# Cross-attention block with feed-forward on one core: a third pair of keys leads, and the start of the attention stage is ordered anew

## The reference, cut to what matters

```python
h = layernorm(x)                                   # (8, 128, 512)
q = rmsnorm(h, ln_weight) @ w_q.T                  # 32 heads x 128
k, v = ctx @ w_k.T, ctx @ w_v.T
score = einsum('bqhd,bkhd->bhqk', q, k) + position_bias[None]
p = softmax(where(mask, score, -inf)); p = where(mask, p, 0)
x = x + h + einsum('bhqk,bkhd->bqhd', p, v) @ w_out.T
xf = layernorm(x)                                  # then the routed feed-forward
x = x + (xf * in_scale) @ sign(weight).T * out_scale + bias
```

## Time and profile before

| | us |
|---|---|
| median of 3 runs | 875.49 (874.83 to 876.92) |
| the profiled execution, its own time | 873.7 |
| its span | 871.9 |
| TensorE busy | 843.1 |
| VectorE / ScalarE / GpSimd busy | 633.6 / 389.2 / 288.1 |

### The profile page before, as it was taken

One profiled execution on the slowest core, in us unless ns is written; L12 is line 12 of the kernel. 1 busy time (PEld: TensorE's weight loads), 2 busy tenths in 40 slices (PEclk: granted clock), 3 DMA queues, 4 the chain that ended last, 5 costly groups with the idle time before them and its releaser, 6 DMA issues.

```text
span 871.9 us, 12869 instructions
## 1 busy us (share of the span) xinstructions
PE 843.1 (97%) x4348; PEld 706.0 (81%) x4348; DVE 633.6 (73%) x1019; ACT 389.2 (45%) x1005; POOL 288.1 (33%) x279
## 2 busy tenths in 40 slices
PE   9889999999899998799999999999999999999897
PEld 8778888888778876688888888888888888888775
DVE  5966746846877696777777777777777787789755
ACT  5623413413332352445544554555555445556542
POOL 0211111111011024244545445544454355433236
PEclk9999999999999999999999999999999999999969
DMA  8173553555453648242144224413431342150002
GB/s 305 68 230 121 184 202 109 174 213 157 151 170 133 204 145 277 103 148 98 58 151 149 66 89 148 142 49 116 148 105 66 135 149 97 59 206 7 1 0 97
DMA packets 58656, 114.07 MB, mean 131 GB/s; under 512 B 5192, under 2 KB 34760, under 8 KB 53344
## 3 DMA queue, kind: packets, MB, share of 16 engines
q1 hardware_dynamic: 58592, 113.25, 37.7%
HBM read 77.58 MB, written 35.65 MB: 130 GB/s over the span
## 4 chain that ended last, share of the span: by engine, by line
PE 79%; DVE 11%; DMA 3%; ACT 3%; issue 2%; POOL 1%; SPq 0%; POOLq 0%; DVEq 0%; ACTq 0%
PE out L1207 9%; PE out L1209 9%; PE out L1208 9%; PE proj L1207 8%; PE proj L1209 8%; PE proj L1208 8%; PE o L1298 6%; PE s L1279 6%; PE t L1287 3%; PE s L1207 3%; PE s L1209 3%; PE s L1208 2%; DVE w_lo L941 2%; DMA w_stage<-in_wk 2%; DMA w_stage<-in_wq 2%
## 5 line engine op out<-in xcount | busy, mean ns | idle before, releaser
L815 ACT ACTIVATE probs<-probs,neg_max 128x128 f32<-128x128 f32 x256 | 99.8, 391 | 145.4 <-DVE neg_max L1074 145.3
L667 POOL TENSOR_TENSOR w_stage<-w_stage 128x256 f32<-128x256 f32 x30 | 22.5, 749 | 342.5 <-DMA w_stage<-in_wk 275.2
L1097 DVE TENSOR_TENSOR acc<-out,acc 128x512 f32<-128x512 f32 x128 | 87.4, 688 | 41.7 <-PE out L1209 41.1
L679 POOL TENSOR_TENSOR w_lo<-w_stage,w_hi 128x512 fp32r<-128x512 f32 (+1 forms) x52 | 60.0, 1165 | 135.0 <-ACT w_hi L753 135.0
L1207 PE MATMUL out<-wo_hi,o_hi 128*128 128x512 f32 x224 | 95.2, 425 | 0.7 <-DVE acc L1097 0.6
L1207 PE MATMUL proj<-x_hi,w_hi 128*128 128x512 f32 x210 | 88.9, 423 | 2.0 <-DVE w_lo L941 1.5
L1209 PE MATMUL out<-wo_lo,o_hi 128*128 128x512 f32 x224 | 88.0, 393 | 0.0
L1208 PE MATMUL out<-wo_hi,o_lo 128*128 128x512 f32 x224 | 87.6, 391 | 0.0
L1209 PE MATMUL proj<-x_lo,w_hi 128*128 128x512 f32 x210 | 82.5, 393 | 0.0
L1208 PE MATMUL proj<-x_hi,w_lo 128*128 128x512 f32 x210 | 82.1, 391 | 0.0
L753 ACT ACTIVATE w_hi<-w_stage 128x512 fp32r<-128x512 f32 (+1 forms) x113 | 62.0, 566 | 39.7 <-POOL w_stage L669 26.2
(11 more groups left out here) (317 smaller groups left out, 2130.0 us busy)
## 6 DMA issues: line engine op xcount, KB each, us to landing
k_spill<-ring SPq DMA_DIRECT2D x64, 256.0 KB, 2.8
v_spill<-ring SPq DMA_DIRECT2D x64, 256.0 KB, 2.2
w_stage<-in_wk SPq DMA_DIRECT2D x32, 256.0 KB, 3.1
big_stage<-in_wv SPq DMA_DIRECT2D x8, 1024.0 KB, 8.2
w_stage<-in_wq SPq DMA_DIRECT2D x32, 256.0 KB, 4.1
k_first<-k_spill SPq DMA_DIRECT2D x8, 1024.0 KB, 7.1
v_first<-v_spill SPq DMA_DIRECT2D x8, 1024.0 KB, 4.8
k_second<-k_spill SPq DMA_DIRECT2D x8, 1024.0 KB, 7.1
```

The costliest lines, as they stand in the source:

```text
L679: pool.tensor_tensor(lo, w_stage[:, STAGED[part]], hi.bitcast(F32), ALU.subtract).then_inc(g_wlo, 1)
L815: last = act.activation(probs[:, j % 2, b, :], probs[:, j % 2, b, :], ACT.Exp, bias=neg_max[:, col:col + 1], accum_out=row_sum[:, col:col ...
L1097: dve.tensor_tensor(acc[:, b, :], out_bank[n % 2][:], acc[:, b, :], ALU.add).then_inc(v_acc, 1)
```

## The change

It touches the order of steps and a few buffers. Nothing is computed in another way.

- **A third pair of keys leads:** the groups are K0 K1 K2, then V V K V V K K three times, then the last four value groups in a row, then K12 to K15 and the queries. Loads, sums and splits of pair 2 move ahead of the values' load and splits.
- **Two staged blocks have two places:** `w_stage` has ten blocks; for odd pairs the second block of row 1 and the last sum lie in 8 and 9 instead of 6 and 7. Row 1 of pair m now waits for the sums of pair m - 1 and for part 3 of pair m - 2; GpSimd's sums wait for part 2 of pair m - 1.
- **Value sums are own steps** (VS, g, n), in three slots; **roots are own steps** of ScalarE (LNR, RMSA), behind LN and RMS by some slots.
- **x:** H writes into the x tile itself; x loads 4 to 7 wait for transposes 0 to 3. Transposes 0 to 3 stand beside the first of the last value groups. Keys and values of pair 0 are loaded in cycle 30 instead of 31.
- **The first units:** score 1, transpose 0 and EXP 1 stand inside cycle 33; units 1 to 4, with the products of groups 33 and 34 beside them, have an order written out.
- **Memory:** `bias_raw` moves behind `probs`; its first two loads wait for the x splits.

```diff
-    order = KEYS[0:2]
-    for g in range(NVG):
-        k = 2 + 3 * g
+    order = KEYS[0:3]
+    for g in range(NVG - 1):
+        k = 3 + 3 * g
...
-    return order + KEYS[14:] + QUERIES
+    return order + VALUES[-HALF:] + KEYS[-4:] + QUERIES
...
-        k = weights_at(m)
-        near = m > 0 and weights_at(m - 1) == k - 1
-        if m:
-            put(k, 4 if near else 1, ("WX", m + 1, 0))
+        near = m > PLAIN and weights_at(m - 1) == weights_at(m) - 1
+        k = weights_at(m) + {PLAIN: 2, PLAIN + 1: 1}.get(m, 0)
+        put(k, 4 if near else 1, ("WX", m + 1, 0))
         put(k, 6 if near else 5, ("WX", m + 1, 1))
         put(k + 1, 1, ("WX", m + 1, 2))
         if m <= NPAIR:
-            put(k + 1, 0, ("WL", m + 2, 0))
-        put(k + 1, 2, ("WX", m + 1, 3))
-        if m <= NPAIR:
-            put(k + 1, 2, ("WL", m + 2, 1))
-            put(k + 1, 4, ("WS", m + 2))
...
+            put(k + 1, 0, ("WL", m + 2, 1), ("WL", m + 2, 0))
+            put(k + 1, 3, ("WS", m + 2))
+        put(k + 1, 5 if m == NPAIR else 2, ("WX", m + 1, 3))
+
+    put(2, 0, ("VS", 0, 2))
+    put(2, 2, ("VX", 0, 6))
+    put(2, 4, ("WX", 2, 3), ("WL", 3, 1), ("WL", 3, 0))
+    put(2, 6, ("VX", 0, 2))
+    put(3, 0, ("CT", "T4"), ("CX", 4))
+    put(3, 2, ("VX", 0, 5))
+    put(3, 4, ("VS4", 0), ("VX", 0, 7))
+    put(4, 0, ("WS", 3), ("VX", 0, 3))
+    put(4, 2, ("VX", 0, 4))
+    put(4, 4, ("VL", 1))
+    put(6, 0, ("VS", 1, 0))
+    put(6, 3, ("VS", 1, 1))
+    put(6, 6, ("VS", 1, 2))
...
-    put(k - 6, 6, ("LN", 0))
-    put(k - 5, 1, ("RMS", 0))
-    put(k - 5, 4, ("RMSR", 0))
...
+    put(k - 7, 2, ("LN", 0))
+    put(k - 7, 6, ("LNR", 0))
+    put(k - 6, 1, ("RMS", 0))
+    put(k - 6, 4, ("RMSA", 0))
+    put(k - 6, 6, ("RMSR", 0))
...
+    for i in range(HALF):
+        put(k, i, ("X", i), ("XL", HALF + i))
+    put(k, 6, ("LN", 1))
+    put(k + 1, 2, ("LNR", 1))
...
+    put(k + 4, 0, ("XX", 1))
+    put(k + 4, 2, ("XT", "T1"), ("XX", 2))
+    put(k + 4, 5, ("XT", "T2"), ("XX", 7))
...
+    put(k + 6, 5, ("KV", 0), ("BL", 0), ("BL", 1))
+    q = at[QUERIES[0]]
+    put(q, 5, ("BM", 0), ("BM", 1))
+    put(q, 6, ("KV", 1), ("WOL", 0))
+
+    put(q + 1, 0, ("S", 0), ("EXP", 0), ("SMALL",))
+    put(q + 1, 3, ("N", 0), ("BL", 2))
+    put(q + 1, 4, ("S", 1))
+    put(q + 1, 6, ("T", 0), ("EXP", 1), ("BM", 2))
...
+             ("WX", 2, 0), *plain_read(1, "C11"), ("WX", 2, 1), *plain(1, "C12", 0), *plain(1, "C12", 1), ("CX", 5), *plain_read(1, "C21"),
+             ("WX", 2, 2), *plain(1, "C22", 0), *plain(1, "C22", 1), ("VX", 0, 1), ("VS", 0, 0), ("VS", 0, 1), ("CX", 7),
+             *plain_read(1, "C12"), *plain_read(1, "C22")]
...
-            steps += slot(j, product(first, 7) + prod[1], product(first, 3), [], [("WX", m, 2)])
-            steps += slot(j + 1, prod[6] + product(first, 4), prod[2], [("WO", p)], [("WX", m, 3)])
...
+            steps += [*product(first, 7), *prod[1], ("WX", m, 2), ("N", 1), ("PV", 0), ("RES", 0), ("RES", 1)]
+            steps += [("S", 2), *product(first, 3), ("T", 1), ("EXP", 2), ("BM", 3), ("BL", 3), *prod[6], ("N", 2), ("PV", 1),
+                      ("WO", 0), ("RES", 2), ("RES", 3)]
+            steps += [("S", 3), *product(first, 4), *prod[2], ("WX", m, 3), ("T", 2), ("EXP", 3), ("BM", 4), *prod[5], ("N", 3),
+                      ("PV", 2), ("WOL", 1), *load, ("RES", 4), ("RES", 5)]
+            steps += [("S", 4), *prod[7], *prod[3], ("T", 3), ("EXP", 4), ("BM", 5), ("BL", 4), ("RES", 6), ("RES", 7), *prod[4],
+                      *outs(0, 0), ("N", 4), ("KV", 2), *sums, ("PV", 3), *outs(0, 1, 2)]
...
+                else:
+                    sp.wait_ge(g_wsum, 4 * (m - PLAIN))
+                if m > PLAIN and row == 0:
                     sp.wait_ge(*low_done(m - 1, 0))
                     sp.wait_ge(*low_done(m - 1, 1))
-                    sp.wait_ge(g_wsum, 4 * (m - PLAIN))
-                else:
-                    sp.wait_ge(*low_done(m - 1, 2))
-                    sp.wait_ge(*low_done(m - 1, 3))
...
+                if m > PLAIN + 1 and row == 1:
+                    sp.wait_ge(*low_done(m - 2, 3))
...
+                    to = w_stage[:, 5:9:3] if m % 2 else w_stage[:, 5:7]
...
             def x_load(i):
                 if i >= HALF:
-                    sp.wait_ge(v_hs, i - HALF + 1)
+                    sp.wait_ge(pe_x, i - HALF + 1)
...
+                if m > PLAIN:
+                    pool.wait_ge(*low_done(m - 1, 2))
```

More of the change, by code:

```diff
@@ new lines, in schedule @@
+            put(k + 5, 5, ("VS", g + 1, 1))
+            put(k + 6, 1, ("VS", g + 1, 2))
+    k = at[VALUES[-HALF]]
+    put(k - 9, 3, ("ML",))
+    put(k - 9, 5, *[("XL", i) for i in range(HALF)])
+    put(k - 8, 3, ("MASK",))
+    put(k - 7, 2, ("LN", 0))
[3 more added lines that the diff above has]
+    put(k - 6, 6, ("RMSR", 0))
+    put(k - 5, 2, ("H", 0))
+    put(k - 5, 5, ("H", 1))
+    put(k - 4, 1, ("H", 2))
+    put(k - 4, 5, ("H", 3))
@@ new lines, in schedule @@
+    for i in range(HALF):
+        put(k, i, ("X", i), ("XL", HALF + i))
+    put(k, 6, ("LN", 1))
+    put(k + 1, 2, ("LNR", 1))
+    put(k + 1, 3, ("RMS", 1))
+    put(k + 1, 5, ("RMSA", 1))
+    put(k + 2, 0, ("RMSR", 1))
+    put(k + 2, 2, ("H", 4))
+    put(k + 2, 4, ("H", 5))
+    put(k + 2, 5, ("X", 4))
+    put(k + 2, 6, ("H", 6))
+    put(k + 3, 0, ("X", 5))
+    put(k + 3, 1, ("H", 7))
+    put(k + 3, 2, ("X", 6))
+    put(k + 3, 4, ("X", 7), ("AL",))
+    put(k + 3, 6, ("XT", "T3"))
@@ L485, in split_tiles, with staged @@
             return w_hi[:, PARTS[part]], w_lo[:, PARTS[part]]
+        def staged(m, part):
+            if part == 3:
+                return w_stage[:, 8:10] if m % 2 else w_stage[:, 6:8]
+            return w_stage[:, (slice(0, 1), slice(1, 3), slice(3, 5))[part]]
         def ctx_low_done(i):
@@ L615, in bias_load @@
             def bias_load(i):
-                if i >= 2:
+                if i < 2:
+                    sp.wait_ge(a_xhi, 7)
+                    sp.wait_ge(v_xlo, 7)
+                else:
                     sp.wait_ge(g_bm, max(j for j in range(len(UNITS)) if bias_of(j) == i - 2) + 1)
@@ L678, in query_weights_low @@
                 pool.wait_ge(a_whi, nth_split[m, part])
-                pool.tensor_tensor(lo, w_stage[:, STAGED[part]], hi.bitcast(F32), ALU.subtract).then_inc(g_wlo, 1)
+                pool.tensor_tensor(lo, staged(m, part), hi.bitcast(F32), ALU.subtract).then_inc(g_wlo, 1)
             def bias_and_mask(j):
@@ L746, in weights_high @@
                     before = m - 2
-                if before < PLAIN:
+                if m == PLAIN:
+                    act.wait_ge(pe_plain, all_plain // 2 if part < 2 else nth_plain[1, part - 2, 0, 1])
+                elif before < PLAIN:
                     act.wait_ge(pe_plain, all_plain)
@@ L752, in weights_high @@
                             act.wait_ge(pe_prod, nth_product[group_with(before), i])
-                act.activation(hi, w_stage[:, STAGED[part]], ACT.Copy).then_inc(a_whi, 1)
+                act.activation(hi, staged(m, part), ACT.Copy).then_inc(a_whi, 1)
             def values_high(g, i):
@@ L940, in key_weights_low @@
                 dve.wait_ge(a_whi, nth_split[m, part])
-                dve.tensor_tensor(lo, w_stage[:, STAGED[part]], hi.bitcast(F32), ALU.subtract).then_inc(v_wlo, 1)
+                dve.tensor_tensor(lo, staged(m, part), hi.bitcast(F32), ALU.subtract).then_inc(v_wlo, 1)
             def values_low(g, i):
@@ L1039, in normed @@
                 dve.wait_ge(v_hs, i + 1)
[L1040 to L1044 removed]
+                dve.scalar_tensor_tensor(out=x_tiles[:, i % HALF, :], in0=hs_tile, scalar=rrms[:, i:i + 1],
                                          in1=lnw_bc, op0=ALU.mult, op1=ALU.mult).then_inc(v_h, 1)
```

120 lines of the change are left out of this document (36 added, 84 removed).

## The result

The changed kernel takes **870.28 us** (median of eight runs, 868.79 to 873.62), the kernel before 876.66 on the same chip (872.78 to 877.90). The ratio is 0.9943, 95% interval 0.9921 to 0.9964: faster, by 6.4 us (0.7%) in the medians. The forecast was 858 with a range of 854 to 868, so the sign was right and the gain was a third of what I had worked out.

What follows compares the result with a forecast made beforehand. TensorE, busy 97% of the span, was taken as the bound, so only its idle time could go: 22.7 us at most, less 4.9 lost anew, gives 17.8. From 873.7 that is 855.9 profiled, 858 median, range 854.3 to 868.

Steps and rivals of the forecast that it cites:

- The 22.7 us that could be won: Ceiling on the gain: TensorE's waits ahead of 385 us, with restarts and slow clock, in the profiled execution before.
- The start: Third key pair leading: 1.6 us lost as VectorE has no slack and meets GpSimd's pair sums (bounds 0.4 and 4).
- The waits of the value sums: Later value groups: with sums in separate slots, the 2.5 us wait for E65 and two short waits (0.9) go.
- the root: ScalarE's root, moved 3 to 4 slots after its source, no longer holds up E1; TensorE's 2.5 us loss goes.
- The new wait of the pair sums: Rival, attention stage: later sums make each of 14 pairs' weights late, 22 us come back, 880 us; chance 0.03.
- land 9.5 to 10 later ... 1.0 lost (bounds 0 and 3): First query product: weight rows of pair 16, queued behind 2 MB of keys and values, cost 1.0 us.
- the loads behind keys and values come late: Rival: 2 more at the first query, 3 more at unit 0, 1.7 of clock, 864.5 us; chance 0.12.
- Walking it from the start of group 33 ... I take 1.5 lost; bounds 0.4 and 6: First attention units in their new order: small waits, a late load and restarts cost 1.5 us.
- By hand E65 of it ends 0.9 ahead of need. I leave 0.1; keep 2 as the upper bound.: Group 28, x sums and splits pushed together on VectorE: its read E65 still in time, 0.1 us lost.
- both middle rivals: VectorE becomes the bound in pressed stretches (863.5 us, chance 0.18); loads behind keys and values late (864.5, chance 0.12).
- over 8 us of waits ahead of 385: Sign in the changed profile: TensorE waits totalling more than this before 385 us would show the forecast wrong.
- a wait of over 1 us after 400: Sign in the changed profile: one such TensorE wait would show the forecast wrong.

Runs made afterwards that it cites:

- e8: The kernel before with value sums and roots as own steps and nothing else; 871.32 us against 876.16, ratio 0.9935.
- e1: The changed kernel with keys, values and bias of pair 0 issued behind the two rows of weight pair 16; 864.26 us, ratio 0.9859 to the kernel before.
- e5: The kernel of e4 with the second keys, values and output weights also issued behind the rows of weight pair 18; 856.86 us, ratio 0.9771.
- e3: The changed kernel with GpSimd's low split of output weights 0 moved behind bias and mask 4; 870.62 us, ratio 0.9926 to the kernel before.
- e9: The changed kernel with the low split of the first output weights moved from GpSimd to VectorE; 866.77 us, ratio 0.9919 to the kernel before.
- e2: The changed kernel with the eight residual scalings moved from between the units into cycles 31 and 32; 864.29 us, ratio 0.9854 to the kernel before.
- e6: The kernel of e5 with the last block sum of x moved to slot 4 and its split to slot 6 of cycle 30; 857.01 us, ratio 0.9774.
- e4: The changed kernel with the edits of e1 and e2 together; 859.18 us, ratio 0.9802 to the kernel before.

## Why the prediction was wrong in size

**What was right.** The 22.7 us that could be won, from the earlier trace rows, were won, to about 1 us: the account closes within 0.2, of which 1.0 is luck in the feed-forward part. The start lost 1.6, as taken. The waits of the value sums (2.5 and 0.9) and of the root (2.5) went as said; e8, with these steps alone, won 4.8 by the medians and 5.7 by the ratio. The statistics cost less than the 0.5 left for them. The first PV runs without a wait and at the full clock. VectorE was no bound up to 300 us. The new wait of the pair sums cost nothing in the attention stage, where the windows of 20 us from 380 to 760 have TensorE busy for 20.00, but for 19.97 in one.

**Which steps failed.**

- *"land 9.5 to 10 later ... 1.0 lost (bounds 0 and 3)."* It was 4.3, and 2.2 of clock. Two errors. The one row on record for this queue said 10.6 from issue to use with 2 MB ahead, and I took less, although row 1 and two loads of the bias were now queued as well; it measured 11.4. And I had the issue 0.5 ahead of group 31; it came 1.3 behind the first product of that group (311.77 against 310.47). These two make 1.6 and 1.8 of the error. Behind the load the splits stand in a chain: ScalarE's split of the row, then GpSimd's sums, then parts 1 and 2. From ScalarE's split to the product it took 1.2, where I had 0.8. The rival "the loads behind keys and values come late" had this mechanism and the clock too, but priced it at 6.7 and gave it 0.12. It measured 4.3 + 2.2 at the first query and 1.4 at unit 0; e1 and e5 together give that back (6 and some 2.5).
- *"Walking it from the start of group 33 ... I take 1.5 lost; bounds 0.4 and 6."* It was 7.8. I listed the new order of the units and never walked the RES steps in it. They moved from 334 to 354, where VectorE had time, to 356 to 375, where the read of every product is wanted. A moved step counts with every instruction and in its new company: eight scalings at 0.54 look like 4.3 us hidden on an engine with slack, and they met GpSimd's 2.40 us. I had used the exclusion of VectorE and GpSimd at the start (1.76 instead of 1.23), found the rule of the Trainium skill ("SBUF — State Buffer") too strict there, and applied neither here. In this knot a scaling took 2.54. That reading of the start was wrong too. I had added the whole 0.75 of a GpSimd sum to the 1.23 of the split. What is added is only what is left of the other instruction when the second one comes. Ahead of the sum at 23.52 GpSimd ran

```profile
21.96 1.60 POOL L669 TENSOR_TENSOR w_stage<-w_stage 128x256 f32<-128x256 f32 x1
```

which ends at 23.56, 0.68 after the start of the split at 22.88. Full exclusion gives 0.68 + 1.23 = 1.91 for it, and the trace has 1.76; for the sum at 23.52, which meets the split until 24.64, it gives 1.12 + 0.75 = 1.87, and the trace has 1.71. Both rows are within 0.2 of the rule, and don't speak for a weaker one.
- *"By hand E65 of it ends 0.9 ahead of need. I leave 0.1; keep 2 as the upper bound."* It was 1.7. The late one was not E65 of group 28 but a weight split of group 30, behind ScalarE's 3.8 us of standing for a block sum. Some 1.0 of the wait is this packing, and it stays where no GpSimd sum is met (e3, e9). The other 0.4 is that the block sum of 1.23 took 1.75 beside GpSimd; I had not laid GpSimd's sums of the pair beside group 30.

**The range.** Its upper end, 868, is about the sum with every term at its upper bound (4 + 0.2 + 0.5 + 3 + 2 + 6 = 15.7 against 4.9, so 857.7 + 10.8 = 868.5). (The reason given with it, both middle rivals and half of their sum, does not come to 868: half of 5.5 + 6.7 on top of 858 is 864, all of it is 870.) Two terms came out above their bounds, 6.5 against 3 and 7.8 against 6. The first bound was passed by the wait alone (4.3) and had nothing for the clock, which was left to a rival; the second had a late load and a fall of the clock in it, and nothing for the scalings. And the two middle rivals (5.5 and 6.7 more) were each priced as if the other could not happen; both at once are 870.

**The signs.** I had named over 8 us of waits ahead of 385 as what would show me wrong. They are 11.4. The other sign, a wait of over 1 us after 400, was badly chosen: the kernel before has one of 2.15 at 808.70, in the last transposes, and so has the changed kernel.

**What is open.** The clock's share of e1's and e2's gains was not measured by itself. Why the last 44 us of an execution vary by up to 1.7 us was not asked. What one place costs with keys and values behind row 1 of the weights has no run. Whether row 1 of the weights, put on another queue than SP, would end the lateness without moving keys and values was not tried.

The best version is e5 (and e6, which cannot be told from it): 856.86 us, 2.3% below the kernel before and 13 us below the changed kernel, with three groups of steps moved (the two loads of keys and values with what goes with them, and the scalings).

## What to carry to other kernels

When steps are reordered, write down for each moved load what is queued ahead of it in bytes, and take the time from issue to first use from the worst like row of the trace, not a bit less. When steps are moved onto a shared engine, count the ones that look free too, and lay the queue of the other engine beside them: here a VectorE instruction that touched only SBUF took its own time plus what was left of the GpSimd instruction it met (2.54 us instead of 0.54). A gain made early is kept only if every later knot can take the earlier time; look for the knots first, and treat their chances as one chance. Before reading a gain of 1 us from two spans, compare the two traces at an instruction ahead of any stretch that the change doesn't touch.

## What the runs showed of the hardware

- A scaling of 128x512 on VectorE (fp32, SBUF to SBUF) takes 0.54 us by itself and took 2.54 beside a GpSimd subtraction of 128x1024 that takes 2.40. Sums and splits with two SBUF inputs took 1.75 instead of 1.23, and GpSimd's sums 1.61 and 1.71 instead of 0.74, in the same stretch: both sides wait, each for about what is left of the other. A read of PSUM beside such a sum (309.32, with the sum at 308.26) stayed at 0.68. With the subtraction on VectorE (e9) it took 1.22 there, half of its time on GpSimd, with no GpSimd instruction beside it, and the scalings behind it took 1.00 for two.
- The length of a stop alone does not tell whether TensorE's granted clock falls. It fell to its lower level after the stop of 4.3 us, after 1.4 and 2.9 within 7 us (0.58 at 373 to 377), in e2 after one of 2.98 (0.52 at 322 to 326), and in e4 after one of 1.84 (0.69 at 346 to 350). It stayed at 1.00 after 1.88 and 2.25 in the kernel before, and in e9 after one of 2.99.
- 256 KB loads issued 2.0 and 1.4 us behind the first of 2 and 2.5 MB on the same queue were in use 9.4 and 10.4 us after their own issue (11.4 and 11.8 after the large ones went out). The page of the changed kernel's profile gives 4.4 us from issue to landing as the median of such loads.
